# A fused attention kernel: probabilities moved once in f32, value matmuls with V stationary in four column tiles

## What is computed

```python
a1 = _attn(q, k1, v1, causal=True)      # latent keys and values
a2 = _attn(q, ks, vs, causal=False)     # 32 selected tokens
a3 = _attn(q, kw, vw, causal=True)      # keys and values projected from x
g = gate[:, :, None, None, None]
out = g[:, 0] * a1 + g[:, 1] * a2 + g[:, 2] * a3
out = out.transpose(0, 2, 1, 3).reshape(B, T, N_HEAD * V_HEAD)
return out @ w_proj
```

## Time and profile before

| | us |
|---|---|
| median of 3 runs | 2240.78 |
| lowest, highest | 2236.99, 2243.73 |
| profiled execution | 2239.67 |
| its span, first to last instruction | 2237.9 |

### The profile page before, as it was taken

One profiled execution on the slowest core, in us unless ns is written; L12 is line 12 of the kernel. 1 busy time (PEld: TensorE's weight loads), 2 busy tenths in 40 slices (PEclk: granted clock), 3 DMA queues, 4 the chain that ended last, 5 costly groups with the idle time before them and its releaser, 6 DMA issues.

```text
span 2237.9 us, 48381 instructions
## 1 busy us (share of the span) xinstructions
PE 1905.6 (85%) x13756; PEld 1306.6 (58%) x13756; DVE 1669.0 (75%) x4134; ACT 1382.1 (62%) x4244; POOL 879.9 (39%) x851
## 2 busy tenths in 40 slices
PE   4334346899989998999999999999999999999996
PEld 2212223667666766676666666666666666666762
DVE  5999952777777777677868776877687768887882
ACT  1112212677767776777767776777677767676771
POOL 0232324444434443454445434543554245434500
PEclk7655665999999999999999999999999999999997
DMA  4000001111111111111111211121112111211101
GB/s 138 0 0 0 0 2 45 44 37 45 35 44 35 40 41 45 34 36 45 44 35 35 47 44 35 35 47 44 35 35 47 44 34 35 47 44 33 36 2 38
DMA packets 71388, 81.76 MB, mean 37 GB/s; under 512 B 29521, under 2 KB 37842, under 8 KB 70994
## 3 DMA queue, kind: packets, MB, share of 16 engines
q1 hardware_dynamic: 71122, 78.55, 13.6%
HBM read 7.70 MB, written 2.10 MB: 4 GB/s over the span
## 4 chain that ended last, share of the span: by engine, by line
PE 70%; DVE 17%; issue 7%; ACT 3%; POOL 1%; SPq 1%; DVEq 0%; DMA 0%; ACTq 0%; POOLq 0%
PE bank L1582 23%; PE bank L1609 12%; PE bank L1483 4%; PE bank L1599 4%; PE bank L1600 4%; PE bank L1484 3%; PE bank L1584 2%; DVE arena L1311 2%; PE bank L1434 2%; PE bank L1541 2%; PE bank L1525 2%; DVE arena L1306 1%; PE bank L1479 1%; DVE arena L1074 1%; PE bank L1548 1%
## 5 line engine op out<-in xcount | busy, mean ns | idle before, releaser
L1582 PE MATMUL bank<-arena 96*128 96x512 f32 (+6 forms) x2048 | 779.1, 462 | 32.2 <-issue 22.3
L1306 DVE TENSOR_REDUCE arena<-bank 128x1 f32<-128x512 f32 (+3 forms) x1024 | 498.4, 487 | 375.0 <-PE bank L1584 365.8
L856 ACT ACTIVATE arena<-bank 128x512 f16<-128x512 f32 (+3 forms) x1024 | 449.3, 439 | 335.8 <-PE bank L1609 321.8
L876 ACT ACTIVATE arena<-bank,arena 128x512 f32<-128x512 f32 (+3 forms) x1024 | 541.8, 529 | 116.0 <-DVE arena L1306 103.9
L1609 PE MATMUL bank<-W,arena 128*128 128x128 f32 x2560 | 475.8, 284 | 46.8 <-ACT arena L876 24.6
L1311 DVE TENSOR_TENSOR arena<-bank,arena 128x512 f16<-128x512 f32 (+3 forms) x1024 | 493.1, 482 | 4.1 <-ACT arena L856 3.5
L1582 PEld LDWEIGHTS bank<-arena 96*128 96x128 f32 x2048 | 332.3, 196 | 150.8 <-issue 137.2
L1599 PEld LDWEIGHTS bank<-arena 128*128 128x128 f16 x2560 | 239.5, 98 | 179.3 <-issue 118.4
L1600 PE MATMUL bank<-arena 128*128 128x96 bf16 x2560 | 338.4, 205 | 0.0
L1599 PE MATMUL bank<-arena 128*128 128x96 bf16 x2560 | 337.5, 205 | 0.9 <-DVE arena L1311 0.9
L1609 PEld LDWEIGHTS bank<-W,arena 128*128 128x128 f32 x2560 | 279.6, 143 | 77.5 <-issue 38.5
(11 more groups left out here) (265 smaller groups left out, 2833.2 us busy)
## 6 DMA issues: line engine op xcount, KB each, us to landing
arena<-arena SPq DMA_DIRECT2D x896, 64.0 KB, 2.0
arena<-arena SPq DMA_DIRECT2D x64, 128.0 KB, 2.2
W<-wide SPq DMA_DIRECT2D x1, 3538.0 KB, 12.9
X<-x SPq DMA_DIRECT2D x8, 256.0 KB, 5.6
out<-arena SPq DMA_DIRECT2D x8, 256.0 KB, 2.2
arena<-arena SPq DMA_DIRECT2D x96, 16.0 KB, 1.9
LW<-lat SPq DMA_DIRECT2D x1, 768.5 KB, 13.9
arena<-mods SPq DMA_DIRECT2D x1, 768.0 KB, 4.5
```

The costliest lines, as they stand in the source:

```text
L856: A(PTh[:, k % 4, 0:n], bank[3 + k % 2][:, 0:n], ACT.Copy).then_inc(s_hi, 1)
L876: A(Pb[:, s % 4, 0:n], bank[s % 3][:, lo:lo + n], ACT.Exp, bias=nmax[:, s:s + 1], accum_out=lsum[:, c:c + 1]).then_inc(s_p, 1)
L1306: v.tensor_reduce(nmax[:, s:s + 1], bank[s % 3][:, lo:lo + n], AX_X, ALU.max, negate=True).then_inc(s_max, 1)
L1582: MM(bank[s % 3][:, 0:lo + n], query(t), Kb[a][0:QD, g % 2, h, skip:skip + lo + n], start=True, stop=False)
```

## The change

- **Order of the units.** HALVES = ((3, 2), (1, 0)): for each attention first tiles 3 and 2 of all four heads (a tall half), then tiles 1 and 0 of all four (a low half). A row is now 16 units (RU), one attention of a group.
- **One move.** The transposed probabilities are copied once, in f32, into PT (one buffer for tall halves, one for low ones): tile 2 by ACT (step s - 2), tiles 3, 1 and 0 by DVE (step s - 3). The fp16 pair is gone.
- **Value matmuls.** V is f32, read out of bank 7 straight into place by ACT, and is now the stationary operand (32 columns); the probabilities are the moving one. The four heads write 32 partitions each of bank 5, in four column tiles. A row has six calls of four heads: key blocks 0 to 3 of the tall half in steps 11 to 14 (PV_TALL; 256, 256, 256 and 128 columns), 0 and 1 of the low half in steps 19 and 20 (PV_LOW; 256 and 128), that is in steps 3 and 4 of the next row. `split_values` is gone.
- **Norm.** The output comes out transposed, so the inverse row sums have to lie along the free axis. DVE inverts 16 columns of sums times the gate (step 16), POOL repeats each 32 times (`repeat`), PE transposes the result in four pieces into bank 6 (`spread`, step 19), ACT moves it (step 21), DVE multiplies all four heads by it (step 23) and adds the two attentions (step 24).
- **Fills.** ocT is gone, since the output already is transposed; o2 is one matmul of 512 columns, read by DVE as an addition.

```diff
-TILES = (3, 1, 0, 2)
+HALVES = ((3, 2), (1, 0))
-T_LAG, L_LAG, V_LAG = 2, 3, 5
+T_LAG, D_LAG = 2, 3
+PV_TALL, PV_LOW = 11, 19
+INVERT, SPREAD, MOVE, NORM, ADD = 16, 19, 21, 23, 24
+MOVER = {3: "dve", 2: "act", 1: "dve", 0: "dve"}
...
+            def repeat(turn, r):
...
+                row = inv[:, r % 2].rearrange("p (n o) -> p n o", o=1).to_broadcast([P, NT * HG, VH])
+                pool.tensor_tensor(ivX.rearrange("p (n v) -> p n v", v=VH), row, ones_hv, ALU.mult).then_inc(s_ix, 1)
...
-                        A(PTh[:, k % 4, 0:n], bank[3 + k % 2][:, 0:n], ACT.Copy).then_inc(s_hi, 1)
+                        positive(s_pv, turn.half_free(k))
+                        A(turned(turn, k), turned_bank(turn, k), ACT.Copy).then_inc(s_pa, 1)
...
-                        TT(PTl[:, k % 4, 0:n], bank[3 + k % 2][:, 0:n], PTh[:, k % 4, 0:n], ALU.subtract).then_inc(s_lo, 1)
...
+                        CP(turned(turn, k), turned_bank(turn, k)).then_inc(s_pd, 1)
...
+                    for h in range(HG):
+                        rows = slice(h * VH, (h + 1) * VH)
+                        last = MM(bank[5][rows, low * 2 * P:low * 2 * P + n], V[a][turn.g(q) % 2][:, c, rows],
+                                  PT[low][:, h, c * 2 * P:c * 2 * P + n], start=(c == 0), stop=(c == top))
...
+                    for n in range(NT):
+                        last = pe.transpose(bank[6][:, n * P:(n + 1) * P], ivX[:, n * P:(n + 1) * P], ident)
...
-                            MM(out, PTh[:, k % 4, c * P:(c + 1) * P], parts, start=(c == 0), stop=False)
-                            last = MM(out, PTl[:, k % 4, c * P:(c + 1) * P], parts, start=False, stop=(c == t))
```

More of the change, by code:

```diff
@@ L45 @@
 LAT_N = DQ_N + 1
-TILES = (3, 1, 0, 2)
+HALVES = ((3, 2), (1, 0))
 def units(groups):
-    return [(q, h, a, t) for q in range(groups) for a in range(2) for h in range(HG) for t in TILES]
+    return [(q, h, a, t) for q in range(groups) for a in range(2) for half in HALVES for h in range(HG) for t in half]
 def scores_at(a, t):
@@ L82, in group_tasks @@
     if not first:
-        out += [(steps["ocT"], "ocT", q - 1), (steps["op"], "op", q - 1)]
+        out += [(steps["op"], "op", q - 1)]
     if not (last and g == NG - 1):
@@ L144, in col, with half_free, moved @@
     def col(self, s):
-        return s - s % NT + self.units[s][3]
+        q, h, a, t = self.units[s]
+        return s - s % RU + (NT - 1 - t) * HG + h
+    def half_free(self, k):
+        r = self.r0 + k // RU
+        return r * 2 - 1 if self.units[k][3] >= 2 else r * 2
+    def moved(self, k, who):
+        per = sum(MOVER[u[3]] == who for u in units(1))
+        if k < 0:
+            return self.p0 * per - sum(MOVER[u[3]] == who for u in units(1)[k + 1 + GU:])
+        return self.p0 * per + sum(MOVER[u[3]] == who for u in self.units[:k + 1])
 class Steps:
@@ L704, in _ @@
             rope(turn, "k", 1)
-            split_values(turn, 1)
+            repeat(turn, 0)
+            repeat(turn, 1)
             rope(turn, "q", 2)
             rope(turn, "k", 2)
-            split_values(turn, 2)
+            for r in range(2, (NG - 1) * GR):
+                repeat(turn, r)
             norm_out(B - 1)
@@ L771, in positive @@
             def positive(sem_, value):
-                if not (isinstance(value, int) and value == 0):
+                if not (isinstance(value, int) and value <= 0):
                     act.wait_ge(sem_, value)
@@ new lines, in row_normed @@
+                def row_normed(r):
+                    q, a = divmod(r, GR)
+                    v.wait_ge(s_pv, (r0 + (r + 1)) * 2)
+                    v.wait_ge(s_iv, r0 + (r + 1))
+                    if a == 0 and not turn.first:
+                        v.wait_ge(s_g, turn.filled("op", q - 1))
+                    TT(wcT if a else ocT, bank[5][:], ivT, ALU.mult).then_inc(s_nrm, 1)
+                def row_added(r):
+                    q, a = divmod(r, GR)
+                    if a == 1:
+                        v.wait_ge(s_nrm, r0 + (r + 1))
+                        TT(ocT, ocT, wcT, ALU.add).then_inc(s_comb, 1)
```

237 lines of the change are left out of this document (124 added, 113 removed).

## The result

| | before, us | after, us |
|---|---|---|
| median of 4 runs | 2241.48 | 2285.59 |
| lowest, highest | 2236.99, 2243.73 | 2280.42, 2289.40 |
| profiled execution, its span | 2239.67, 2237.9 | 2280.42, 2278.6 |

The changed kernel takes 1.0198 of the time before (95% interval 1.0172 to 1.0224): 2.0% slower, where 1.7% was forecast.

What follows compares the result with a forecast made beforehand. PE was taken to bound the attention loop. The span of 2237.9 us, +64 of PE work, -26 of waits, 1.8 around it and 1.1 to the median make 2279 us; 8 in 10 from 2218 to 2335.

Steps and rivals of the forecast that it cites:

- main case: Whole kernel: the forecast of 2279 us holds, within 2245 to 2308 us; chance 0.60.
- The calls: New value matmuls on PE: 12 calls a group, 8 x 0.76 + 4 x 0.54 = 8.2 us, replacing 6.7 us.
- The fixed price: Cost of each four-tile value call on PE besides its columns: 0.33 us, between ends of 0.26 and 0.36.
- Net -0.8 a group: PE's waits in the loop: 0.6 us a group new, 1.4 gone, together -26 us.
- 1.4 of 1.75: PE's waits on busy DVE, ACT or POOL: 1.4 of 1.75 us a group should go as those engines get lighter.
- What the order in halves costs: Pairs of units without a value call or fill, in low and tall halves: some 0.6 us a group of new PE waits.
- rival A: Low halves: short pairs and long DVE stretches expose PE, waits grow 0.7 us a group, 2327 us; chance 0.20.
- The loop's branch: At the loop's branch, the chain after the last score takes 3.6 us against 3.5 before: no change.
- B: Value calls: the fixed price isn't paid; faster below 0.23 us a call, 2210 us at 0.15; chance 0.16.
- C: Value calls: the column tiles don't overlap, 17.1 us a group and not 4.3, 2689 us; chance 0.02.
- D: Clock: low halves' waits bring a fall below full speed into every group, 7 us each, 2447 us; chance 0.02.
- PE busy at 96% or more: Sign expected in the profile after: PE busy at least 96%, with a period of 57.6 us a group.

Runs made afterwards that it cites:

- run 5: Changed kernel with transposes and ACT's copy three steps behind the scores, not two, value calls one step later, DVE's copy unmoved: 2245.63 us, ratio 1.0017 to before.
- run 3: Kernel before without DVE's subtraction of the low half; value matmuls take the high half twice, waiting for ACT's high half instead: 2186.69 us, ratio 0.9766.
- run 6: Run 5 with the value calls of a half also issued back to back in one step: 2205.16 us, ratio 0.9842 to the kernel before.
- 1: Changed kernel with all value calls of a half issued back to back in one step, not one per step: 2289.06 us, ratio 1.0212 to before.
- 2: Changed kernel with the fill o2 moved from step 24 (25) of a group to step 29: 2298.38 us, ratio 1.0257 to the kernel before.
- 8: Run 6 with the turn of the normed heads (z4T) moved from step 17 to 19, once a batch: 2203.19 us, ratio 0.9840 to before.
- 12: Run 5 with DVE's copy one step later too, four steps behind the scores: 2332.71 us, ratio 1.0412 to the kernel before.

## Why the prediction was right in its time and wrong in its waits

- **The sum.** 2279 was forecast, 2285.6 measured, inside the main case (2245 to 2308). 57.6 us a group were forecast, 57.8 came. Two terms were off, in opposite directions, so that the nearness is in part luck. (DVE's passes that go add up to 841.2 us and not 841.6; nothing hangs on it.)
- **The calls: mechanism right, size a little off.** 8 x 0.715 + 4 x 0.502 = 7.7 us a group for 8.2. The fixed price was read from fills, and 0.29 came for 0.33. Four tiles start within 0.03 us and run side by side. On PE's own work the change costs -6.7 + 7.7 + 0.46 = +1.5 us a group, not +2.0.
- **The waits: the step that failed.** "Net -0.8 a group" was the forecast. In the six whole batches PE's idle time rose from 10.6 to 13.7 us a batch, 0.8 a group more; 0.45 of that is the loop's branch (below). The period rose by 1.8 a group where 1.2 was forecast, and 1.5 of it is PE's own work. The views of PE's waits between 400 and 2150 us (us in total, times, longest) show the parts, before:

```profile
PE bank L1609 <- ACT arena L876: 23.0, 33, 3.4
PE bank L1609 <- DVE arena L1311: 20.9, 34, 2.0
PE bank L1434 <- DVE arena L1218: 3.5, 7, 0.5
```

and after:

```profile
PE bank L1660 <- DVE arena L1338: 29.3, 48, 0.8
PE bank L1462 <- DVE arena L1246: 15.1, 7, 2.2
```

The waits of the transposes fell by a third (43.9 to 29.3), where four fifths of all waits were to go (1.4 of 1.75). And a wait grew that the sum did not have: the turn of the normed heads (z4T, L1434 before and L1462 after), once a batch. In the second batch after, PE had one transpose, at 865.63, to put against a fixed stretch of DVE:

```profile
865.91 2.06 DVE L1246 TENSOR_SCALAR arena<-X,small 128x128 f32 x4
868.11 0.64 PE L1462 MATMUL bank<-W,arena 128*128 128x128 f32 x4 [2.15 <-DVE arena L1246]
```

What the order in halves costs was put at 0.6 from chains of short pairs. No run changes the order alone in the new kernel; as an estimate of what one step of slack takes away there, run 5 gives 40 / 32 = 1.25. The waits sit less in the plain pairs than where a fixed DVE stretch (o2's read, z4T) stands ahead of what PE needs. That was rival A's mechanism, which I had priced as an alternative (+1.5 a group) instead of as a part of the sum. The other half, 1.4 back from lighter engines, has no run of its own: run 3 gives 53 / 32 = 1.65, but with a step of slack beside the lighter DVE.

- **The loop's branch: "nothing" was wrong.** PE's idle time put down to issue is 33.1 us in six pieces, 22.3 in six before, so 1.8 each. It was 31.8 to 37.2 in all seven runs made from the changed kernel, and 15.5 to 27.8 in those of the old one. DVE has such a gap of its own at the same place: it ends the last group's work at 1370.26 and starts its next at 1373.30. What the gaps are made of was not settled.
- **Left out:** the first groups and the tail (+2.8, -6.1), which no term covered.
- **DVE, ACT, POOL.** A copy from PSUM costs what a subtraction of its width did: (174.3 + 106.3 + 71.9) / 32 = 11.0 us a group, as forecast. The totals, 33.5 and 33.2, are some 2 above the forecast 31 and decide nothing.
- **The rivals.** B fails by its own bound: 0.29 is above the break-even of 0.23. The new layout wins only with the calls side by side and the step of slack (run 6). C and D are refuted: 0.57 us for a call of 256 columns, and a clock of 0.97 in the batch window. But the prediction had misread the trace before in D: the clock fell not only about the branch, but in two of the six whole batches for 3.4 us in the third group too, and after in all six. One of each (windows; the clock is the last but two):

```profile
1000.60:1004.00 3.40, 3.40 (x22) 3.16 (x20) 2.91 (x12) 1.69 (x5) 0.00 (x0) 0.51 0.06 10
1013.70:1017.11 3.41, 3.41 (x24) 1.31 (x23) 2.69 (x11) 0.50 (x3) 0.00 (x0) 0.50 0.05 10
```

- **The signs.** Calls, DVE, ACT and the period came as forecast or near it. "PE busy at 96% or more" did not: 221.65 of 235.60 us are 94%, less than the 95.6% of the earlier trace rows. It was the sign that looked at all waits of PE, and it shows that they had not fallen.

The 0.74 for slower held, but for reasons that happened to balance: had the calls cost the forecast 0.33, the time would have been 15 us higher.

## What to carry to other kernels

When a change makes an engine lighter and changes the order in which its work arrives, cost the two together: the order that cost 46 us in the old kernel cost nothing once the subtraction, and the wait for it, were gone. In a hand-ordered pipeline ask how many steps lie between the release of a buffer and its next use, and what the releasing instruction stands behind; one step of slack was worth 40 us here, and moving a single fill, tried twice, was worth nothing. Before moving a lag, look for a second engine that must hand the result on in the same step. An experiment that takes work off an engine often also changes who frees a buffer; count that step too. Compare the granted clock of every pair of runs before explaining their difference. And a saving on the bounding engine should be tried again once its waits are gone: the same edit gave 0 and then 40 us.

## What the runs showed of the hardware

- A step into column tiles and out again costs 0.29 us (0.09 before, 0.14 inside, 0.055 behind), the same at 128 and at 256 columns, and calls that follow each other pay it once: four took 1.65 us for 1.49 of columns.
- The mean granted clock of a whole execution differed between programs with the same number of matmuls on PE: 0.893 to 0.913 in the changed kernel and runs 1, 2, 5, 6, 8 and 12, which is 198 to 249 us missing from full speed.
- PE's idle time at the end of a loop's pass differed between programs of nearly the same work there: 3.7 us each in the old kernel, 5.5 in the new one.
